# A graph layer whose 128-row gathers are issued as two, of 122 rows and of 6

## What is computed

```
m_in     = concat(x[src], x[dst], edge_attr)        # 400000 x 144
h        = silu(m_in @ W1 + b1)                     # 144 -> 64
messages = silu(h @ W2 + b2)                        # 64 -> 64
agg      = segment_sum(messages, dst, 12500)
node     = silu(concat(x, agg) @ W3 + b3)           # 128 -> 64
out      = layernorm(x + node)
```

## Time and profile before

| | |
|---|---|
| timed runs | 5670.6 and 5712.9 us, median 5691.8 |
| span of the profiled execution | 5651.1 us, 40.7 us below that median (its own launch time is not given apart) |
| busy, share of the span | PE 67%, POOL 51%, PEld 40%, DVE 31%, ACT 19% |
| gathers (L356) | 2975, 2863.2 us in all |
| granted TensorE clock, mean | 0.80 of full |
| DMA | 24 GB/s on average |

### The profile page before, as it was taken

How to read it: one execution, slowest core, us unless ns; L and a number is a source line. 1 busy time by engine, 2 the same in 40 slices (tenths; PEclk the granted TensorE clock), 3 DMA queues, 4 the chain that set the end, 5 groups by cost and what they waited for, 6 DMA issues and landing times.

```text
span 5651.1 us, 67318 instructions
## 1 busy us (share of the span) xinstructions
PE 3790.3 (67%) x21762; PEld 2256.6 (40%) x21972; DVE 1750.0 (31%) x4664; ACT 1063.5 (19%) x1975; POOL 2864.2 (51%) x2983
## 2 busy tenths in 40 slices
PE   3556667766767776666766676676667776766676
PEld 1333334443434444333433344444334443443444
DVE  2332233322323333232332333233233332332333
ACT  1111111211212112111121212111111121211212
POOL 5555544554554555444555454454544554444552
PEclk6667778887888888788887888787888777887788
DMA  2111111110111111011111111111110110111110
GB/s 59 25 26 23 23 22 22 25 24 21 25 24 22 22 26 23 22 22 22 24 24 23 22 22 23 22 26 22 23 23 21 25 24 21 23 22 22 24 23 17
DMA packets 281731, 135.07 MB, mean 24 GB/s; under 512 B 180684, under 2 KB 233709, under 8 KB 281700
## 3 DMA queue, kind: packets, MB, share of 16 engines
q0 software_dynamic: 95200, 97.68, 7.8%
q1 hardware_dynamic: 172690, 33.68, 3.0%
q10 hardware_dynamic: 13810, 3.35, 0.3%
HBM read 131.24 MB, written 3.20 MB: 24 GB/s over the span
## 4 chain that ended last, share of the span: by engine, by line
PE 42%; another core or an unknown queue 27%; issue 16%; DVE 8%; ACT 4%; DVEq 3%; ACTq 0%; DMA 0%; SPq 0%
PE pick_ps L898 20%; PE agg_ps L846 8%; PE in_ps L813 7%; PE z_ps L836 3%; PE z_ps L830 2%; DVE msg L599 2%; DVEq L573 2%; ACT msg L428 2%; DVE in_T L594 2%; PE pick_ps L885 1%; ACT rows_T L468 1%; PE agg_ps L825 1%; DVE edge_in L702 1%; DVE kept L694 1%
## 5 line engine op out<-in xcount | busy, mean ns | idle before, releaser
L356 POOL DMA_INDIRECT edge_in<-in_x_dram,src_i x2975 | 2863.2, 962 | 2725.2 <-DMA src_i<-in_src_dram 1653.3
L898 PE MATMUL pick_ps<-parts,rows_T 128*128 128x512 bf16 (+1 forms) x5640 | 1503.2, 423 | 780.2 <-issue 437.5
L898 PEld LDWEIGHTS pick_ps<-parts,rows_T 128*128 128x128 bf16 x5850 | 589.5, 109 | 1689.4 <-issue 925.1
L846 PE MATMUL agg_ps<-edge_in,msg 128*64 128x48 f32 x6256 | 556.3, 253 | 443.5 <-ACT msg L428 288.8
L830 PE MATMUL z_ps<-in_T,w_in 128*64 128x512 f32 x782 | 507.0, 735 | 470.3 <-DVE w_in L596 293.6
L846 PEld LDWEIGHTS agg_ps<-edge_in,msg 128*64 128x64 f32 x6256 | 503.2, 167 | 770.4 <-ACT msg L428 495.9
L599 DVE TENSOR_TENSOR msg<-z_ps,b_rep 128x512 f32<-128x512 f32 x391 | 269.1, 688 | 1712.8 <-remote 1562.8
L420 ACT COPY in_T<-in_ps 128x512 f32<-128x512 f32 x391 | 229.2, 586 | 1996.7 <-PE in_ps L813 1013.5
L813 PE MATMUL in_ps<-ident,edge_in 128*128 128x128 f32 x3128 | 538.0, 324 | 52.6 <-issue 46.2
L428 ACT ACTIVATE msg<-msg,zero_col 128x512 f32<-128x512 f32 x391 | 282.2, 722 | 1387.6 <-DVE msg L599 1324.5
L831 PE MATMUL z_ps<-in_T,w_in 128*64 128x512 f32 x782 | 507.6, 736 | 0.0
(11 more groups left out here) (88 smaller groups left out, 1664.7 us busy)
## 6 DMA issues: line engine op xcount, KB each, us to landing
edge_in<-in_x_dram,src_i POOLq DMA_INDIRECT x2975
ea<-in_edge_attr_dram SPq DMA_DIRECT2D x390, 64.0 KB
src_i<-in_src_dram SPq DMA_DIRECT2D x390, 4.0 KB
dst_i<-in_dst_dram SPq DMA_DIRECT2D x390, 4.0 KB
out_dram<-result ACTq DMA_DIRECT2D x15, 192.0 KB
dst_g<-in_dst_dram SPq DMA_DIRECT2D x1, 1536.0 KB
out_dram<-result ACTq DMA_DIRECT2D x1, 224.0 KB
b_col<-in_L_gnn_b_dram ACTq DMA_DIRECT2D x4, 0.2 KB
```

Of the source, the lines that this page charges most:

```text
L356: pool.indirect_dma_start(out=edge_in[:, to_slot, t, XS], out_offset=None, in_=x[:, :], in_offset=bass.IndirectOffsetOnAxis(ap=indices[:, ...
L846: last = nc.tensor.matmul(agg_ps[H:P, nodes], msg[:, t % HT, t // HT, :], edge_in[:, s, t, nodes], start=(t == 0), stop=(t == T - 1))
L898: last = nc.tensor.matmul(pick_ps[r][:, 0:(b - a) * H], rows_T[:, c, :], parts[:, i, a:b, :].rearrange("p k f -> p (k f)"), start=(c == 0 ...
```

## The change

The kernel gets a second index buffer, `cut_i`, of six partitions, and a semaphore for each slot of it. From the seventh group on, SP loads the last six rows of the group's index block into it, right behind the load of `src_i` and ahead of `dst_i`. POOL waits for both loads. It then issues, for each tile of the group, a gather of partitions 0 to 121 by `src_i`, and after all of these, for each tile, a gather of partitions 122 to 127 by `cut_i`. Each of them counts 16 on the slot's semaphore, so PE waits for twice the count of such a group. The first 48 gathers and the last five stay whole. The data that arrive are the same.

```diff
+        CUT = 122
         src_i = sb("src_i", [P, S, T], I32)
+        cut_i = sb("cut_i", [P - CUT, S, T], I32)
...
+        s_cut = [sem(f"src_rows_moved{s}") for s in range(S)]
...
                         sp.dma_start(src_i[:, s, :], src_v[k * S + s]).then_inc(s_src[s], 16)
+                        sp.dma_start(cut_i[:, s, :], src_v[k * S + s][CUT:P, :]).then_inc(s_cut[s], 16)
                         load_rest(k, k * S + s, s)
...
+            def gather_cut(slot, tiles, arrived):
+                for t in range(tiles):
+                    pool.indirect_dma_start(
+                        out=edge_in[0:CUT, slot, t, XS], out_offset=None, in_=x[:, :],
+                        in_offset=bass.IndirectOffsetOnAxis(ap=src_i[0:CUT, slot, t:t + 1], axis=0),
+                    ).then_inc(arrived, 16)
+                for t in range(tiles):
+                    pool.indirect_dma_start(
+                        out=edge_in[CUT:P, slot, t, XS], out_offset=None, in_=x[:, :],
+                        in_offset=bass.IndirectOffsetOnAxis(ap=cut_i[:, slot, t:t + 1], axis=0),
+                    ).then_inc(arrived, 16)
...
                         pool.wait_ge(s_src[s], k * 16 + 16)
+                        pool.wait_ge(s_cut[s], k * 16)
                         pool.nop(nofuse=True)
-                        gather(src_i, s, s, PICKED if s in picked else T, s_xg[s])
+                        gather_cut(s, PICKED if s in picked else T, s_xg[s])
...
-                        gathered = k * (16 * T * TURNS) + 16 * T * (turn + 1)
+                        gathered = k * (32 * T * TURNS) + 32 * T * (turn + 1) - 16 * T
...
-                            gathered = j * (16 * (T * TURNS - each)) + 16 * (T * (FIRST + turn) - now)
+                            gathered = j * (32 * (T * TURNS - each)) + 32 * (T * (FIRST + turn) - now) - 16 * T
...
-                    gathered = T * (g // S) + (TT if g == FULL else T) - each * (BODIES - ITERS)
+                    gathered = 2 * T * (g // S) - T + (TT if g == FULL else 2 * T) - 2 * each * (BODIES - ITERS)
```

## The result

The changed kernel takes **9459.91 us**, the median of two runs (9456.98 to 9462.84), beside 5691.77 before: 1.663 times as long, with a 95% interval of 1.651 to 1.676. That is 1990 us beyond the forecast and 1160 beyond the top of its range.

What follows compares the result with a forecast made beforehand. The prediction took POOL's issuing as the changed kernel's bound: 92.8 us to the first pair, 2922 x 2.50 = 7305, five whole gathers 6.3, 24 at the end, span 7428; with 40.7 more, 7470 us. Range 6100 to 8300.

Steps and rivals of the forecast that it cites:

- Bound by POOL: POOL's issuing of gather pairs bounds the changed kernel from its first pair on: 2922 x 2.50 = 7305 us; chance 0.55.
- The 40.7 us between span and time: Added to the predicted span of 7428 us, because the timed median of before lay 40.7 us above its span.
- The 122-row half: On POOL, the gather of rows 0 to 121: 1.25 us with its gap, like the 128-row gather.
- the 6-row half: On POOL, the gather of the last six rows: taken at 1.25 us with its gap, bounds 0.40 and 1.25.
- B: Rival: PE hardly moves beside gathers, its pace falling below 0.53; at 0.40, 260 us a body and 8450 us; chance 0.07.
- C: Rival: gathers on fewer queues make pairs short and cure PE's late signals, down to 4590 us; chance 0.16.
- Rival A: The short half is cheap on POOL: at 0.40 us a pair is 1.65, in all 6150 us; chance 0.22.
- PE's pace: PE is busy 0.53 beside gathers and 0.87 without; each us of longer gathers costs a body 0.39 us.
- the 2.33 us: The time of a pair from which POOL's issuing, 212 us a body, becomes the bound.
- What PE could do: PE at 0.87 throughout takes 119.2 / 0.87 = 137 us a body.
- SP's fourth load: One more DMA for each of 384 groups, 190 us of SP's time, hidden in its 3124 us of waiting for PE.
- the DMA engines: Queue 0 uses 7.8% of them; another 32 packets for a pair don't fill them.

Runs made afterwards that it cites:

- cuts of 120 and 122: The kernel before with gathers from the seventh group on fetching only rows 0 to 119, or 0 to 121: 5481.12 and 5977.96 us, before 5706.67.
- 120 cut: The changed kernel with gathers cut at row 120 and not 122: 9480.82 us, before 5741.85.
- kernel of six cuts: The changed kernel with each of the six slots cut at another row (64, 112, 120, 124, 125, 126): 9401.61 us, before 5706.67.

## Why the prediction was wrong

**Bound by POOL: right**, from the first pair on. The last gathers of 122 and of 6 rows start 41 and 31 us ahead of the end, PE waits for rows as it did not before, and POOL's waits for indices went from 1653.3 us to about 30. The form of the sum, pairs times price and some 120 us around them, gives the span when the right price stands in it. The 40.7 us between span and time did not belong in it: here they are 2 us apart (9460.7 and 9462.84), and the 40.7 were a difference between executions.

**The step that failed** is "The 122-row half: 1.25 us with its gap, by the row of the 128-row gather, which it nearly is". It measured 1.714 + 0.30 = 2.01 us, by 2922 of them. 2922 x (1.714 - 0.947) = 2241 us are missing from the sum for that, and the 6-row half, taken at 0.95 and measured at 0.873, gives 2922 x 0.074 = 216 back: 7470 + 2241 - 216 = 9495, 0.4% from the result, and most of that 0.4% is the 40.7. The instruction goes by the rows on its fullest queue, 61 instead of 8, as the cuts of 120 and 122 (995 and 1698 ns) show. The range failed with it: I bounded the unknown half on both sides, and gave the half that "nearly is" a whole gather no bounds at all, although no row showed one. The remark in B that a dearer 122-row half "would end here too" had the right cause and no price.

**How many rows a queue gets.** By the Trainium skill, page "DMA: Bandwidth & Descriptors", section "Anatomy of one DMA", many descriptors come before more of them cost anything. The traces agree for 128 rows, where 16 x 8 items at 0.825 ns are 0.1 of 0.95 us, and disagree for 122, where 16 x 61 items are 0.8 of 1.66 us. The prediction took 122 rows for fewer items than 128; the packets show 976 where the whole gather has 128. The rule of 2 and 6 queues, which I weighed in C, holds. I drew from it that fewer queues might be cheaper. It could have been drawn the other way, 61 rows in a line on each, and that was the sign of it.

**Rival A** had the short half at 0.10 us at the least. It measured 0.873, nearly the whole gather: a fixed 0.86 by the line through the cuts.

**Rival C** was half right: the late signals were cured (49.9 us of "remote"), but for the spacing that the dear half brings and, by the trace, because PE's work falls beside that half, not for the number of queues, and the price went up and not down. Without the first half of C the second is worth nothing, since POOL is then the bound.

**A second step was wrong and hidden by the first: PE's pace**, 0.53 beside gathers, entered the forecast only through the 2.33 us from which POOL decides. For the kernel as changed this did no harm, which is luck: the dear half is also the one that spaces the gathers. With the pair at 2.46 us, almost what I had assumed, the 120 cut takes 9480.82, not 7470. More gathers close together make the signals later (36 us at the longest instead of 13), POOL then stops for slots, and a body takes 292 us. This is B's "PE hardly moves", far beyond the 0.40 that I gave it. The argument against B, that the stops are counted in the 0.53, failed: they were counted for the runs of 15 gathers in the earlier trace rows. That it is the length of the runs was not tested apart.

**What PE could do** I read as 0.87, 137 us a body at the clock of before. Without gathers it is 105.8: the granted clock is 0.98 instead of 0.80, the matmuls take 98.1 us instead of 119.2, and PE is busy 0.93 of the time.

**SP's fourth load, the DMA engines and the higher counts** cost nothing, as said: 30 us of waits for indices in all, and 14.9% on queue 0.

## What to carry to other kernels

Before you cut a gather, or any transfer whose descriptors an engine writes, ask how the new count divides: 120 or 126 rows cost a whole tile's time, 122 cost 1.8 times it, and every further instruction a fixed 0.86 + 0.30 us; a size that is "nearly" the measured one is still an unmeasured size, and wants bounds. Where consumers of TensorE's results start late while POOL issues transfers, space those transfers out and measure it: pauses ahead of three in eight gathers made this kernel 0.83 times as long in one series of runs and 1.20 times in another, so compare within a series and repeat it at another time.

## What the runs showed of the hardware that was not expected

- A gather whose rows fall on k of 16 queues gives each of the others as many 4-B items as the fullest has rows: 3416 B for 122 rows, fitting the queue's bytes to 0.01 MB in three kernels, its count of packets exactly in the changed one, and the packets' sizes in those of 122 and 120 rows alone.
- Its time is 859 ns + 0.825 ns x 16 x (rows on the fullest queue), within 5% of all medians measured from 2 to 128 rows. Of 2922 gathers of 122 rows 104 take 0.9 us more and 205 take 0.2 to 0.4 more; why is open.
- TensorE's signals reached VectorE and ScalarE up to 16 us late when gathers started 1.25 us apart, up to 36 when 6,000 of them started 1.15 to 1.28 us apart, up to 51 in the kernel of six cuts, and were prompt (under 1 us) from a spacing of 1.94 us on, or 1.63 on average. In between, at 1.52 on average, they were up to 3.5 us late. In one series of runs they were prompt at 1.25.
- A wait of POOL for its own semaphore takes the gap before the next gather from 0.30 to 0.77 us; a drain sets gathers 3.18 us apart.
